# Criss-cross attention: VectorE takes a score pair's maximum, scale and shift ahead of the projection item and of the other pair's sum

## The reference

```python
q = jnp.einsum('bchw,oc->bohw', x, Wq) + bq[None, :, None, None]
k = jnp.einsum('bchw,oc->bohw', x, Wk) + bk[None, :, None, None]
v = jnp.einsum('bchw,oc->bohw', x, Wv) + bv[None, :, None, None]
eH = jnp.einsum('bchw,bcpw->bhwp', q, k)
diag = jnp.eye(H, dtype=bool)[None, :, None, :]
eH = jnp.where(diag, -jnp.inf, eH)
eW = jnp.einsum('bchw,bchp->bhwp', q, k)
att = jax.nn.softmax(jnp.concatenate([eH, eW], axis=3), axis=3)
attH, attW = (att[..., :H], att[..., H:])
outH = jnp.einsum('bcpw,bhwp->bchw', v, attH)
outW = jnp.einsum('bchp,bhwp->bchw', v, attW)
return gamma.reshape(()) * (outH + outW) + x
```

## Time and profile before

| | |
|---|---|
| median of three runs | 4570.58 us |
| profiled execution: its time / its span | 4574.0 us / 4572.2 us |
| TensorE / VectorE / ScalarE / GpSimd busy | 77% / 65% / 38% / 11% of the span |
| mean granted TensorE clock | 0.85 of full speed |
| one image, first maximum to first maximum of the next (947.24 to 1502.59 us) | 555 us |
| its score stage, first to last maximum (947.24 to 1050.78 us) | 104 us |

### The profile page before, as it was taken

The page is one execution under the profiler, slowest core; times in us unless marked ns, Lnnn a source line. Parts: engine busy times, 40 slices in busy tenths (PEclk is TensorE's granted clock), DMA queues, the critical chain, the costliest instruction groups (busy, mean ns, idle before and its releaser), DMA issues.

```text
span 4572.2 us, 96032 instructions
## 1 busy us (share of the span) xinstructions
PE 3525.7 (77%) x33624; PEld 2418.0 (53%) x33624; DVE 2972.1 (65%) x4282; ACT 1716.7 (38%) x3660; POOL 506.9 (11%) x691
## 2 busy tenths in 40 slices
PE   3986888678876778767788678886787868877676
PEld 2543565445654556545565355563565635655565
DVE  6746775476764866639666386574775747856576
ACT  2434442353423534235242352433433334333431
POOL 0000120001200022000210002100031000300210
PEclk9997798887998789887899878997698986989577
DMA  7967779976889669896698876988769987799489
GB/s 283 299 184 237 245 239 296 290 232 231 271 274 309 211 232 281 264 299 219 217 311 268 272 250 192 338 267 250 261 186 318 292 235 252 204 317 290 148 256 298
DMA packets 753781, 1179.38 MB, mean 258 GB/s; under 512 B 50800, under 2 KB 568432, under 8 KB 744048
## 3 DMA queue, kind: packets, MB, share of 16 engines
q1 hardware_dynamic: 434256, 831.89, 57.7%
q10 hardware_dynamic: 319008, 340.88, 23.1%
HBM read 832.83 MB, written 339.74 MB: 256 GB/s over the span
## 4 chain that ended last, share of the span: by engine, by line
issue 72%; PE 9%; POOL 9%; DVE 4%; DMA 4%; ACT 1%; SPq 1%; POOLq 0%; ACTq 0%; DVEq 0%
POOL qk_lo L455 3%; POOL prob_col L473 3%; POOL prob_row L473 2%; DVE acc L835 2%; PE banks L967 2%; PE banks L969 2%; PE banks L968 2%; DMA v_in<-v_pixel_major 1%; DMA acc<-x 1%; PE banks L1035 1%; DMA out<-acc 1%; PE banks L1037 1%; PE banks L1036 1%; DMA x_first<-x 1%; SPq L361 1%
## 5 line engine op out<-in xcount | busy, mean ns | idle before, releaser
L835 DVE SCALAR_TENSOR_TENSOR acc<-banks,att,acc 128x384 f32<-128x384 f32 x1536 | 1130.0, 797 | 198.9 <-DMA acc<-x 127.2
L967 PE MATMUL banks<-wv_hi,x_hi 128*128 128x512 f16 x2304 | 929.1, 403 | 395.6 <-DVE x_lo L757 394.9
L765 DVE SCALAR_TENSOR_TENSOR v_out<-banks,proj,v_out 128x512 f16<-128x512 f32 x576 | 431.5, 749 | 1134.1 <-ACT v_out L559 1133.5
L968 PE MATMUL banks<-wv_lo,x_hi 128*128 128x512 f16 x2304 | 923.7, 401 | 0.0
L969 PE MATMUL banks<-wv_hi,x_lo 128*128 128x512 f16 x2304 | 919.3, 399 | 0.0
L559 ACT ACTIVATE v_out<-banks,proj 128x512 f16<-128x512 f32 x576 | 390.3, 682 | 859.6 <-PE banks L969 829.2
L1035 PE MATMUL banks<-prob_col,v_in 96*128 96x96 f16 x3072 | 465.5, 214 | 242.1 <-DVE acc L835 236.1
L455 POOL TENSOR_TENSOR qk_lo<-qk_f,qk_hi 128x256 f16<-128x256 f32 x288 | 193.3, 671 | 3567.0 <-ACT qk_hi L567 3559.4
L967 PEld LDWEIGHTS banks<-wv_hi,x_hi 128*128 128x128 f16 x2304 | 235.5, 102 | 663.5 <-issue 456.3
L1035 PE MATMUL banks<-prob_row,v_in 96*128 96x96 f16 x3072 | 456.3, 213 | 101.9 <-DMA v_in<-v_pixel_major 49.8
L1007 PE MATMUL banks<-k_hi,q_both 128*96 128x96 f16 x1536 | 365.1, 295 | 212.4 <-ACT prob_row L606 164.8
(11 more groups left out here) (100 smaller groups left out, 6374.2 us busy)
## 6 DMA issues: line engine op xcount, KB each, us to landing
v_in<-v_pixel_major SPq DMA_DIRECT2D x768, 384.0 KB, 6.0
x_raw<-x ACTq DMA_DIRECT2D x290, 512.0 KB, 7.2
x_next<-x SPq DMA_DIRECT2D x192, 768.0 KB, 4.3
v_pixel_major<-v_out ACTq DMA_DIRECT2D x576, 256.0 KB, 4.0
out<-acc SPq DMA_DIRECT2D x384, 384.0 KB, 10.6
acc<-x SPq DMA_DIRECT2D x192, 384.0 KB, 12.6
acc<-x SPq DMA_DIRECT2D x8, 4608.0 KB, 13.7
acc<-x SPq DMA_DIRECT2D x16, 2304.0 KB, 18.9
```

The lines of the kernel that those rows point to most:

```text
L765: nc.vector.scalar_tensor_tensor(out=v_out[tile % V_OUT][:, :, 1, :], in0=bank[tile % 2][:, :].rearrange("p (t c) -> p t c", t=CT), scalar ...
L835: nc.vector.scalar_tensor_tensor(out=a, in0=out_bank[g % OUTS], scalar=att[:, O_FACTOR:O_FACTOR + 1], in1=a, op0=ALU.mult, op1=ALU.add,).t ...
L967: nc.tensor.matmul(dst, s_hi, m_hi, start=(t == 0), stop=False)
L968: nc.tensor.matmul(dst, s_hi, m_lo, start=False, stop=False)
```

## The change

On VectorE alone, in the loop over the 24 pairs, `score_pair` comes ahead of the item instead of behind it, and `sum_even` of the pair before, which stood inside `score_pair` between the maximum and its scaling, comes behind the item. No instruction is added or removed, and the other engines' order is the same.

```diff
@@ -802,8 +802,6 @@
                     nmax[o][:, both].rearrange("p (u g) -> p u g", u=2), pair_strips[p % 2], AX_X, ALU.max,
                     negate=True,
                 ).then_inc(nmax_raw, 1)
-                if p > 0:
-                    sum_even(b, p - 1)
                 dve.wait_ge(nmax_raw, n + 1)
                 nc.vector.tensor_scalar(
                     nmax[o][:, both], nmax[o][:, both], att[0:L, S_FACTOR:S_FACTOR + 1], None, ALU.mult
@@ -891,9 +889,11 @@
                     if items:
                         item(b + 1, k)
                 for p in range(PAIRS):
+                    score_pair(b, p)
                     if items and p < NP:
                         item(b + 1, HEAD + p)
-                    score_pair(b, p)
+                    if p > 0:
+                        sum_even(b, p - 1)
                     if items:
                         for c in scan_at_pair(p):
                             see_next(b + 1, c)
```

## The result

The changed kernel takes 4535.0 us (median of 4 runs, 4530.5 to 4539.8) against 4570.0 us: a ratio of 0.9924, 95% interval 0.9907 to 0.9942. A second set of six runs gave 4538.4 us, 0.9928 (0.9913 to 0.9943). The forecast was 4539 us.

A forecast was written before the change was run, and what follows sets the result against it. VectorE's order was taken to bound the score stage. Seven images at 3.7 us (25.9) plus 5.8 us for the eighth gave 31.7 us, taking 4570.6 to 4539 us; range 4524 to 4560.

The forecast's parts named there:

- the hole ahead of `low_v`: VectorE's 1.84 us idle in the row pairs, three times an image, waiting for ScalarE's `high_v`; claimed to close.
- The gap: Between each pair's maximum and its scaling, no longer filled by the sum: 0.12 us added to each of 23 pairs.
- Row pairs: From the maximum of pair 0 to that of pair 12: 58.30 us against 61.90, 3.60 us won an image.
- Start: The score stage's first maximum no longer waits behind `low_v`: about 0.95 us won an image.
- Column pairs and the end of the stage: From pair 12's maximum on: 1.32 us lost up to the last maximum, 0.34 us gained back by the last exponentials.
- Eighth image: The image without items or chunk: 4.1 us won in its row pairs, 1.7 in its column pairs, 5.8 in sum.
- ten such steps: Row maxima of the eighth image every 2.51 us instead of 2.92; with the chain's end offset, 4.1 us won.
- (1): Gain given back behind the score stage, where STATS and HEAD wait for DMA: 4571 us, chance 0.08.
- (2): TensorE at its lower clock bounds the row pairs: 4604 us, chance 0.06; weaker form 4550 to 4561, chance 0.10.
- (3): Scaling follows the maximum in 0.86 us, the semaphore costing nothing; 19 us more won: 4520 us, chance 0.06.

## Why the prediction was right

**What bounded the stage: right.** VectorE's order bounded it, and the hole ahead of `low_v` was ScalarE's chain. The chain from exponentials to the end of `high_v` is as long as before (974.05 to 978.14 us, 4.09; before 4.08); only the place at which VectorE asks for its end has moved. Item moved alone closes the hole, sum moved alone doesn't.

**The gap: right, to the hundredth.** The scaling starts 0.98 or 0.99 us behind the maximum in all 192 pairs of the changed kernel. In the kernel before, the sum starts 0.86 us behind it in 161 cases, as many as seven images have. A column pair takes 3.895 us (3.90). The column pairs took 42.85 us with the gap open and 41.48 with the sum in it and no load late. The rule of the Trainium skill ("VectorE: DVE Perf Modes", "The DRAIN you can't avoid"), that the semaphore costs nothing, does not hold for this pair of instructions; without the cost a pair would have taken 3.77 us.

**Row pairs.** 58.15 us, forecast 58.30; won 3.75 an image, forecast 3.60. My account of the 3.60 was loose: I called a remainder of half a microsecond rounding. A hole costs more than its idle note. The note counts from the end of the chunk's maximum, but an instruction behind a full queue starts 1.66 us behind that maximum's start, 0.08 ahead of its end: 975.07 + 1.66 = 976.73 to 978.65 is 1.92 us. Three holes are 5.76, eleven gaps (pair 0 had none filled) 1.32, and the `low_v` of pair 0, which the new order takes inside the stretch, 0.67: 5.76 - 1.32 - 0.67 = 3.77, measured 3.75. The forecast length was 0.15 too long because I took the chunk's maximum as 1.67 us out of column pairs that hold a late load (41.64 us; 41.48 without).

**Start.** The scores' last product of pair 0 ends at 948.27 in the changed kernel and the maximum starts at 948.30, so the start is free of `low_v` as forecast. That these 0.95 us reach the time is shown only in part. The stretch from the last addition to `acc` to the first maximum is 7.7 us shorter in sum than before, and six starts give 5.7 (the seventh lies ahead of the first image's stage, where the profiles vary by 6 us). But the kernel with the sum moved alone, which has no earlier start, has 3101.5 and 3106.3 us between the stages against 3100.8 and 3106.1, so this total is no evidence for the start.

**Column pairs and the end of the stage.** The loss was 1.25 us an image in the mean (forecast 1.32), and 1.37 where nothing else waited (42.85 against 41.48). That the chunk loads never hold up a column pair at 3.785 us was a little too much: in a second profile of the kernel before, three of 84 wait for one, 0.3 to 0.55 us. The residual load is issued before the last maximum starts, where it had been 0.03 us behind it:

```profile
1048.75 0.33 SPq L384 DMA_DIRECT2D acc<-x  x1
```

The last maximum is at 1049.30, so that is 0.55 us ahead of it, 0.58 gained against the maximum, as 0.34 + 2 x 0.12 had it. The time from the last maximum to the first `acc` instruction fell with it, by 3.3 us in seven images (in sum 369.2 before and 365.8 after, means of the profiles). Part of that may be chance: the kernel with the item moved alone, which lacks this step, has 366.0.

**Eighth image: mechanism right, size off by 1 us.** The term of the row pairs was 4.1 us and measured 3.1 (36.3 to 33.1 and 33.3). The step "ten such steps" left out that pair 6 is the first to read the second half of q and k. TensorE and then VectorE at that pair:

```profile
4217.71 0.29 PE L1007 MATMUL banks<-k_hi,q_both 128*96 128x96 f16 x1 [2.39 <-DMA k_lo<-qk_halves]
```

```profile
4219.23 0.95 DVE L801 TENSOR_REDUCE nmax<-banks 96x8 f32<-96x768 f32 x1 [1.55 <-PE banks L1008]
```

The faster pairs now run into a load that was in time in all three profiles of the kernel before: 3.87 us for this step, 2.51 forecast. Its column pairs gained 1.7 us, as forecast.

**The sum.** Stage by stage, from means of the profiles: row pairs 26.3 (25.2), column pairs -8.8 (-9.2), between the stages 12.0 (5.7 from six starts and 2.4 to 4.1 at the end), eighth image 4.8 (5.8), together 34.3 us; the forecast was 31.7, which counts a seventh start. The spans of the profiles differ by 37.0 in the mean; the other 2.7 are nearly all ahead of the first maximum. The run medians give 35.0 and 30.1. That the total is within 4 us is in part luck: the 12.0 can't be put down to its two steps, since the sum moved alone won as much there with one of them, and the eighth image's shortfall stands against the row pairs' surplus.

**The rivals.** (1) fell: the stretches behind the stage did not grow, they shrank. (2) did not occur in the changed kernel, but is nearer than I argued: 2.1 us more delay of x_lo brings it on in part. TensorE's waits for x_lo, worked out as 3.3 us, were 3.36 and 3.21 (rows below). (3) fell with the gap.

## What to carry to other kernels

When an engine bounds a stage and yet has a hole, follow the hole's releaser back: if the chain begins at an instruction of the same engine, put that instruction early and the work that only needs the chain's end late. Count what stood in the way of an instruction as possibly useful: a sum between an operation and the one that waits for its semaphore filled 0.12 us a pair which came back as a cost in every pair without a hole. Choose the order stage by stage, since the same sum was free filling in seven images and a stall in the eighth.

## What the runs showed of the hardware

A scaling on VectorE that waits for the semaphore of the maximum just ahead, and reads what it wrote, starts 0.98 us behind it here, 0.12 us later than the independent sum did; the sum in between hides this. What share the semaphore has in the 0.12 and what the read has, no run separates.

On TensorE's clock, two v items in the changed kernel, behind waits of 3.36 and 3.21 us:

```profile
970.24 0.60 PE L967 MATMUL banks<-wv_hi,x_hi 128*128 128x512 f16 x1 [3.36 <-DVE x_lo L757]
...
984.89 0.39 PE L967 MATMUL banks<-wv_hi,x_hi 128*128 128x512 f16 x1 [3.21 <-DVE x_lo L757]
...
985.76 0.52 PE L968 MATMUL banks<-wv_lo,x_hi 128*128 128x512 f16 x1
986.08 0.63 PE L969 MATMUL banks<-wv_hi,x_lo 128*128 128x512 f16 x1
```

The first item runs at 0.43 us a product from its second product on (granted clock 0.50 from 970.2 to 975 us, the 1.2 GHz level). The second starts at the upper level, its first four products take 0.22 us each (clock 1.00 from 984.8 to 985.7), and the clock falls within the item: 0.50 from 986.1 to 989, 0.43 us a product. The Trainium skill, "TensorE: Matmul & The Clock Gate", section "HAM oscillation", has such waits throttle the array, so that the next burst starts cold, at the lower clock. The rows agree on the throttling both times, and on the cold start only for the first. My remark in rival (2), that not every such wait is followed by slow products, holds in these rows only for the products right behind it: in the kernel before, the wait of 4.13 us that ends at 999.32 has fast scores behind it (clock 1.00 to 999.9), and from 1000.1 us on the clock is 0.50. The clock granted over the row pairs was 0.86 of full speed in the changed kernel, 0.85 before, although x_lo comes later in its pair.
